# Edge data loaded and indexed ahead of the feature chunks in a graph layer; 16 instead of 12 groups gather raw features

## The reference

```python
xn = _layernorm(x)
hx = jnp.einsum('ni,rio->rno', xn, weight)              # 8 relations
agg = jax.ops.segment_sum(hx[edge_type, src], dst, num_segments=6250)
x = x + agg * 0.5 ** 0.5 + h_bias + (xn @ loop_weight) * 0.5 ** 0.5
h = _layernorm(x)
w = (h @ wr + br)[..., 0]
sel = top_k(w, 3125)[:3124]                             # half of the nodes
y = (gelu(h[sel] @ w1 + b1) @ w2 + b2) * w[sel]
x = x + h + (y where selected, else 0)
```

## Time and profile before

| | |
|---|---|
| device time, median of 3 runs | 2123.44 us (2123.23 to 2125.67) |
| profiled execution | 2123.41 us, span 2121.7 us |
| PE busy | 1738.5 us, 82% of the span |
| POOL busy | 1521.4 us, 72% |
| DVE busy | 792.3 us, 37% |
| ACT busy | 728.9 us, 34% |
| gathers | 1598 instructions, 36 of them from x and 1562 from the table |

### The profile page before, as it was taken

One profiled execution on the slowest core, in us unless ns is written; L12 is line 12 of the kernel. 1 busy time (PEld: TensorE's weight loads), 2 busy tenths in 40 slices (PEclk: granted clock), 3 DMA queues, 4 the chain that ended last, 5 costly groups with the idle time before them and its releaser, 6 DMA issues.

```text
span 2121.7 us, 30502 instructions
## 1 busy us (share of the span) xinstructions
PE 1738.5 (82%) x8696; PEld 1476.8 (70%) x8696; DVE 792.3 (37%) x1854; ACT 728.9 (34%) x1511; POOL 1521.4 (72%) x1615
## 2 busy tenths in 40 slices
PE   0599888888888789888888888888888888888882
PEld 0478776777777677777767777776776777777772
DVE  6644333333333433433333343333333334333336
ACT  5543423243233333324323333332333333333242
POOL 6477777777777777777777777777777777777730
PEclk9999999999999999999999999999999999999895
DMA  9943433433433433443343443333333343343336
GB/s 305 326 133 107 125 107 108 126 107 107 127 106 108 124 109 106 117 117 106 117 116 107 116 117 106 116 115 107 117 116 107 112 122 105 107 126 106 105 105 197
DMA packets 126309, 265.87 MB, mean 125 GB/s; under 512 B 32206, under 2 KB 72957, under 8 KB 126138
## 3 DMA queue, kind: packets, MB, share of 16 engines
q0 software_dynamic: 76704, 209.56, 34.2%
q1 hardware_dynamic: 37002, 42.02, 6.1%
q10 hardware_dynamic: 12432, 12.32, 1.7%
HBM read 244.53 MB, written 19.25 MB: 124 GB/s over the span
## 4 chain that ended last, share of the span: by engine, by line
POOL 51%; PE 18%; issue 17%; DVE 4%; DMA 4%; ACT 3%; SPq 1%; DVEq 0%; ACTq 0%; POOLq 0%
POOL messages L474 51%; PE bank L779 7%; PE bank L811 4%; DMA messages<-normed_table,gather_rows 3%; PE bank L832 3%; PE bank L842 2%; SPq L366 1%; DVE acc L1272 1%; PE bank L789 1%; ACT hidden L646 1%; ACT L646 1%; ACT messages L566 1%; PE bank L813 1%; DMA acc<-in_src 0%; DMA w_sb<-in_x 0%
## 5 line engine op out<-in xcount | busy, mean ns | idle before, releaser
L474 POOL DMA_INDIRECT messages<-normed_table,gather_rows x1562 | 1484.3, 950 | 501.4 <-issue 464.3
L779 PE MATMUL bank<-messages,onehot 128*128 128x256 f32 x3196 | 849.3, 403 | 257.9 <-DMA messages<-normed_table,gather_rows 249.5
L779 PEld LDWEIGHTS bank<-messages,onehot 128*128 128x128 f32 x3196 | 588.6, 198 | 369.7 <-DMA messages<-normed_table,gather_rows 293.9
L1115 DVE SCALAR_TENSOR_TENSOR sums<-bank,regular,sums 128x256 f32 x538 | 260.0, 483 | 1220.7 <-PE bank L789 1179.0
L600 ACT ACTIVATE stage<-bank 128x256 f32<-128x256 f32 x538 | 207.6, 386 | 1297.1 <-PE bank L779 1274.0
L811 PE MATMUL bank<-rel_sb,closed 128*128 128x256 f32 x1568 | 355.0, 379 | 0.7 <-ACT closed L608 0.6
L811 PEld LDWEIGHTS bank<-rel_sb,closed 128*128 128x128 f32 x1568 | 297.4, 190 | 42.8 <-ACT closed L608 2.0
L1034 DVE TENSOR_TENSOR onehot<-bank,keys 128x768 f32<-128x768 f32 x269 | 254.6, 947 | 0.1
L832 PEld LDWEIGHTS bank<-normed_t,w_sb 128*128 128x128 f32 x1568 | 222.2, 225 | 6.0
L832 PE MATMUL bank<-normed_t,w_sb 128*128 128x128 f32 x1568 | 218.6, 306 | 0.0
L789 PE MATMUL bank<-ident,stage 128*128 128x128 f32 x1076 | 209.5, 277 | 9.2 <-ACT stage L600 8.7
(11 more groups left out here) (163 smaller groups left out, 634.4 us busy)
## 6 DMA issues: line engine op xcount, KB each, us to landing
side<-normed_table SPq DMA_DIRECT2D x2048, 1.0 KB
messages<-normed_table,gather_rows POOLq DMA_INDIRECT x1562
acc<-in_x SPq DMA_DIRECT2D x12, 512.0 KB
residual<-resid ACTq DMA_DIRECT2D x12, 512.0 KB
node_out<-acc SPq DMA_DIRECT2D x12, 512.0 KB
normed_x<-normed_table ACTq DMA_DIRECT2D x11, 512.0 KB
messages<-residual SPq DMA_DIRECT2D x6, 896.0 KB, 11.1
rel_sb<-in_L_gnn_weight SPq DMA_DIRECT2D x2, 1024.0 KB, 7.5
```

The lines of the kernel that those rows point to most:

```text
L474: pool.indirect_dma_start(messages[0:EP, g % RING, j * D:(j + 1) * D], None, x if g < RAW else table, bass.IndirectOffsetOnAxis(ap=gather_ ...
L779: last = nc.tensor.matmul(banks[g % STAGES][:, 0:D], onehot[0:EP, g % SLOTS, j, :], rows, start=(j == 0), stop=(j == J - 1))
L1115: V.scalar_tensor_tensor(sums[:, :, to], banks[TURNS[g % 2]][:, 0:D].rearrange("p (n m) -> p n m", m=W), regular[:, 0:1], sums[:, :, to], ...
```

## The change

- SP loads dst, type and src right behind src's first tile and the setting of pads, and the chunks of x behind these. The wait for chunk 2 goes.
- Chunks 4 and 5 lie in the areas of src and type within `acc` instead of in `sums`. SP waits ahead of chunk 4 until src has been copied, ahead of chunk 5 until the keys are computed.
- DVE does index, window and order stage ahead of the chunks. Raw batch 0's moments come ahead of the places, its factors behind them.
- ACT clears `sums` first, then copies src and takes all ten tables, then norms the chunks, and then raw batches 0 and 1.
- `RAW` is 16. Groups 12 to 15 form batch 3, in the loop's ticks 8 to 11; groups 14 and 15 lie in ring slots 0 and 1. The statistics keep room for three batches, so batch 3 waits until batch 0 has been normed.
- SP loads w1 and w2 behind the first four blocks of x for `acc`, and the first block waits for these four blocks alone.
- The waits for the small vectors move from ahead of the loop to the first use.

```diff
-    RAW = 12
+    RAW = 16
     RAW_BATCH = 4
+    RAW_KEPT = 3 * RAW_BATCH
...
+    def raw_tiles(k):
+        first = J * RAW_BATCH * k % (J * RAW_KEPT)
+        return slice(first, first + J * RAW_BATCH)
...
-        rel_rows, w1_rows, w2_rows, sums_rows = (rows_of(a[:, :, :]) for a in (rel_sb, w1_sb, w2_sb, sums))
+        rel_rows, w1_rows, w2_rows = (rows_of(a[:, :, :]) for a in (rel_sb, w1_sb, w2_sb))
+        src_rows, type_rows = (edge_area(k)[:, 0:CH * D].rearrange("p (v d) -> p v d", d=D) for k in (0, 1))
         chunk_rows = [rel_rows[:, 0:CH, :], rel_rows[:, CH:2 * CH, :], w1_rows[:, 0:CH, :], w2_rows[:, 0:CH, :],
-                      sums_rows[:, 0:CH, :], sums_rows[:, CH:2 * CH, :], closed_rows[:, 0:CH, :]]
+                      src_rows, type_rows, closed_rows[:, 0:CH, :]]
...
             sp.dma_start(src_s[:, 0, :], src[0:P * GE].rearrange("(p e) -> p e", e=GE)).then_inc(src_first_in, 16)
+            sp.wait_ge(pads_set, 3)
+            for a, to in ((dst, dst_s), (edge_type, type_s)):
...
+            sp.dma_start(src_s[rest:rest + 1, full_tiles, 0:E - NG_FULL * GE],
+                         src[NG_FULL * GE:E].rearrange("(p e) -> p e", p=1)).then_inc(src_in, 16)
...
             for c in range(NCH - 1):
+                if chunk_rows[c] is src_rows:
+                    sp.wait_ge(src_first_ready, 1)
+                    sp.wait_ge(src_f_ready, 1)
+                if chunk_rows[c] is type_rows:
+                    sp.wait_ge(keys_flat, 1)
                 sp.dma_start(chunk_rows[c], x_chunks[c]).then_inc(x_in[c], 16)
...
-            sp.wait_ge(pads_set, 3)
-            sp.wait_ge(x_in[2], 16)
-            for a, to in ((dst, dst_s), (edge_type, type_s)):
...
-            sp.dma_start(w1_sb[:, :, :], w1.rearrange("(k p) h -> p k h", p=P)).then_inc(ffn_w_in, 16)
             sp.dma_start(loop_sb[:, :, :], loop_w.rearrange("(k p) o -> p k o", p=P)).then_inc(loop_in, 16)
-            sp.dma_start(w2_sb[:, :, :], w2.rearrange("(m p) d -> p m d", p=P)).then_inc(ffn_w_in, 16)
...
-            for q in range(NB // QUAD):
+            sp.dma_start(acc[:, 0:QUAD, :], quad(x, 0)[0]).then_inc(x_first_in, 16)
+            sp.dma_start(w1_sb[:, :, :], w1.rearrange("(k p) h -> p k h", p=P)).then_inc(ffn_w_in, 16)
+            sp.dma_start(w2_sb[:, :, :], w2.rearrange("(m p) d -> p m d", p=P)).then_inc(ffn_w_in, 16)
+            for q in range(1, NB // QUAD):
...
             act.wait_ge(consts, CONSTS)
             nc.scalar.activation(deviation[:, :], eps[:, :], ACT.Sqrt)
             take_table(0)
+            for half in range(2):
+                last = nc.scalar.activation(sums[:, :, half * OPEN:(half + 1) * OPEN],
+                                            zero[:, 0:1].unsqueeze(1).broadcast_to([P, KR, OPEN]), ACT.Copy)
+            last.then_inc(sums_clear, 1)
+            act.wait_ge(src_in, 16 * 3)
+            nc.scalar.activation(src_f[:, 1:GT, :], src_s[:, 1:GT, :], ACT.Copy).then_inc(src_f_ready, 1)
+            for n in range(1, 2 * GT):
+                take_table(n)
             deviate_chunk(0)
...
+            for k in range(2):
+                raw_deviate(k)
+                for g in range(RAW_BATCH * k, RAW_BATCH * (k + 1)):
+                    raw_norm(g)
...
+                if g == 9:
+                    raw_deviate(3)
+                if g in (10, 11):
+                    raw_norm(2 * g - 8)
+                    raw_norm(2 * g - 7)
...
+                if groups[0] >= RAW_KEPT:
+                    dve.wait_ge(raw_ready, groups[-1] - RAW_KEPT + 1)
                 for g in groups:
-                    dve.wait_ge(gathered[g], 16 * J)
+                    dve.wait_ge(gathered[g % RING], 16 * tiles_through(g))
...
             ends_stage()
+            index_stage()
+            window_stage()
+            order_stage()
             load_moments(0)
...
             raw_moments_of(0)
-            raw_factors_of(0)
-            index_stage()
-            window_stage()
-            order_stage()
             dve.wait_ge(bad_total, 1)
...
             position_stage()
+            raw_factors_of(0)
             dve.sem_inc(tables_ready, 1)
...
+                if g == 8:
+                    raw_moments_of(3)
+                if g == 9:
+                    raw_factors_of(3)
```

## The result

The changed kernel takes **2108.5 us** (median), beside 2124.4 for the kernel before on the same chip: a ratio of **0.9924, 95% interval 0.9908 to 0.994**, some 16 us or 0.76% faster. The forecast was 2106.0 with a range of 2101 to 2114. The profiled execution took 2108.64 us, its span is 2107.0.

The account below looks back on a forecast made before the run. POOL's gathers at a fixed pitch were taken as the bound: span = start of group 16 + 1943.9 + 86.1. The terms put that start at 74.3 us, not 91.69, so 2123.4 - 17.4 = 2106.0 us, range 2101 to 2114.

Parts of the forecast that it names:

- The frame: On POOL, the span is the start of group 16's gather plus 1943.9 us to the last gather plus 86.1 tail.
- (b): Rival, chance 0.05: PE's wait for side rows at group 47 reaches POOL and becomes the bound, 2116 to 2123 us.
- The terms of the sum: Steps to group 16's start: 9.3 + 13.7 + 6.5 + 25.3 + 0.8 + 1.4 + 16.3 + 1.0 = 74.3 us.
- The last chunk: The 124-row x load: in at 42 to 49 us, costing 0 to 5 us, taken as 1.
- What is late next: On POOL, gaps of about 2 us at group 14 and 5 at group 16; table stored at 60 to 69.
- One more raw batch in the loop: Batch 3 on DVE and ACT at groups 8 to 11 costs nothing; 0 to 2 us if PE is slower.
- Side rows: Ready at 207 to 216 us; PE waits 10 to 19 us for them near group 47, POOL does not.
- slack of 44 us: Ring slack: group 61's gather, first to need group 47's slot, comes 44 us after group 47 is summed.
- (a): Rival, chance 0.17: the last chunk or the edges come in slower, 4 to 9 us of gain lost, 2110 to 2115.
- (c): Rival, chance 0.06: 25-row edge transfers are slow of themselves, edges in at about 30, group 16 at 95, 2127 us.
- (d): Rival: the gain is given back at the end, in the tail behind the last gather; given no chance of its own.
- floor without any gap: With no gap on POOL, group 16 would start at 66.0 us and the kernel would take 2097.7.

Follow-up runs that it names:

- a_side32: The changed kernel with SP waiting until 32 groups have been summed before it issues the side rows: 2132.8 us.
- side runs: Two runs of the changed kernel with SP waiting for 24 or 32 summed groups ahead of the first side row: 2112.3 and 2132.8 us.
- b_split: The kernel before with only the last chunk's 124-row load cut into 112 and 12 rows: 2112.8 us.
- a_sums: The changed kernel with chunks 4 and 5 back in `sums`, and so its clear behind the stored table again: 2122.0 us.
- a_best: The changed kernel with the 124-row load cut, and ACT's copies of groups 0 and 1 and DVE's second one-hot build ahead of raw batch 1: 2103.0 us.
- b_raw16: The kernel before with the edits for RAW = 16 alone: 2125.9 us.

## Why the prediction was right, point by point

**The frame.** Start of group 16, fixed pitch, fixed tail: with the numbers of before it gives the span of every run to 4.4 us, but for a_side32, whose extra 21.7 us stand almost wholly in one gap, where rival (b) puts them. The misses in the changed kernel are 1.3 us at group 16, 0.6 in the pitch, 0.7 in the tail, 2.6 of span. The last two are what executions differ by (tails 84.9 to 87.1).

**The terms of the sum**, forecast against measured: edges in 9.3 and 9.54. Index, window and order stage 13.7 and 23.66 - 9.54 = 14.1. First statistics to first norm 6.5 and 6.6. Seven chunks with the wait for the last 26.3 and 56.51 - 30.24 = 26.3. Raw deviation to raw norm 0.8 and 0.9. To the built one-hot 1.4 and 1.2. To group 16 16.3 and 75.57 - 58.58 = 17.0. Two terms were mis-sized, both taken over as "same instructions, same time": the index work by 0.4, as small DVE instructions took longer (last section), and the last step by 0.7, where DVE's pause ahead of raw batch 1 is 1.25 instead of 0.58 us (last section).

**The last chunk** was forecast at 42 to 49, and a landing after 46 was named as what would be wrong. It landed at 46.09 and 47.84, and at 44.54 and 48.08 in the side runs: its cost was 0.9 us on ACT in the first execution, as taken, and some 2 us more in the second. The premise that it "has only gathers beside it" didn't hold: from 33.81 the stores ran beside it. What it would have cost without them no run shows. By the Trainium skill's rate per engine (DMA: Bandwidth & Descriptors, Specifications) it would have been in before 42 (an estimate of the prediction). The trace shows it later, so the bound from the rows was the better one. That only some engines carry it agrees with the share of 0.45 at 32 to 34 us and with the cut loads; no row counts the engines.

**What is late next.** Group 14 and 16 with gaps of 2 and 5 us: measured 1.46 and 6.10. The first agreement is partly luck: POOL ended group 13 at 60.8 and not at 58.5 (last section), and group 0's sum was about as much later. The table, expected at 60 to 69, came at 68.4, at the late end. POOL was busy with groups 14 and 15 until 69.5, so it was in time for group 16 by 1 us, and it is a near limit: with 12 raw groups it holds group 12.

**One more raw batch in the loop** cost nothing at POOL, as forecast. **Side rows**: PE's wait of 12.82 us was foretold (10 to 19), and that POOL doesn't feel it. The sum for the rows' end was 2 us off (60 to 69 and 37.6 and 107 make 205 to 214, not 207 to 216); they were there at 213.35. The slack of 44 us was that of the old start, though. With group 16 earlier by 16 and PE later, it is 27.6.

**The rivals.** (a), slower chunk or edges: in part, the landing at the late end. (b), side rows: absent, and a_side32 shows from where on it would be there. (c), edge transfers slow of themselves: wrong, 0.46 and 0.39 us when no chunk stands before them. (d), given back at the end: not to be seen, 0.7 us in the tail.

**What the prediction didn't see** is how the gain divides. It read the change as one chain made shorter by moving the edge work. b_split shows that cutting one load, with the order left alone, gives 12.7 us at group 16 where the change gives 16.1, and a_sums that without the chunks' new place the new order keeps only 0.8 of them. It didn't see either that the moved key work slows two gathers, by 2.4 us together (last section). In the changed kernel that is hidden behind group 16's wait of 6.10. It makes the floor without any gap, 66.0 for group 16, too low: in a_best group 16 starts at 69.18 with no gap left.

## What to carry to other kernels

Where one engine runs at a fixed pitch for nearly the whole span, the time is the start of its steady run plus that pitch; follow back what ends that start, and leave the rest, even new waits of 13 us elsewhere, unless they outlast the ring's slack. Before reordering a stream around a slow transfer, look at why it is slow: a row count that divides badly, cut in two, gave most of what the reordering gave (12.7 of 16.1 us at group 16). A buffer that is reused as scratch puts its clear behind the scratch's last reader, so each such place is to be priced with the order, not apart from it.

## What was not expected of the hardware

Two raw gathers of the changed kernel take 2.43 and 1.89 us instead of 0.95. Here they are, and the two passes that DVE makes over the index tables at that time:

```profile
13.72 2.43 POOL L487 DMA_INDIRECT messages<-in_x,gather_rows  x1 [0.30 <-issue]
...
16.45 1.89 POOL L487 DMA_INDIRECT messages<-in_x,gather_rows  x1 [0.30 <-issue]
```

```profile
13.18 2.16 DVE L966 TENSOR_TENSOR acc<-acc,hidden 128x1920 f32<-128x1920 int32 x1
15.37 2.16 DVE L967 SCALAR_TENSOR_TENSOR acc<-acc 128x1920 f32<-128x1920 int32 x1
...
20.43 0.42 DVE L995 TENSOR_SCALAR acc<-acc 128x5 int32<-128x5 int32 x1
```

Each of the two gathers ends 0.81 us after a pass does: 16.15 behind 15.34, and 18.34 behind 17.53. All nine runs with the new order show such a pair, and so does b_split, where the passes start at 47.59 and 49.78 and the gathers that end at 50.56 and 52.76 take 1.83 and 1.89. In the kernel before and in b_raw16 POOL was waiting at that time and had no gather to slow. So these passes hold up a gather that starts beside them, wherever they stand in DVE's stream.

The reverse is seen with small integer instructions on DVE. The first row in the kernel before is the same instruction as the last row above:

```profile
67.75 0.17 DVE L979 TENSOR_SCALAR acc<-acc 128x5 int32<-128x5 int32 x1
...
76.00 4.01 DVE L916 BATCH_NORM_STATS2 hidden<-messages 128x6 f32<-128x256 f32 x12 [0.58 <-issue]
```

It takes 0.42 us at its new place and 0.17 at its old. This and its like make up most of the 0.4 us of the index stage. In the changed kernel it begins while a gather runs (19.91 to 20.85) and ends with it, at 20.85. In all nine runs with the new order this instruction and a second one like it (0.30 at 23.04) end within 0.02 us of a gather that was running when they began; in b_split and b_raw16 no gather was running, and they take 0.17. That points to the gather, though no run takes the gathers away on purpose. Not every instruction is held up: a cast at 20.22 takes 0.17 beside the same gather.

The last row is the start of raw batch 1 in the kernel before, with the pause of 0.58 us that became 1.25. DVE loads a flag there; why that takes longer is open.
